# Moving TensorE's skip products and GpSimd's layer 1 constants inside a four-layer kernel's layer 0 scan

## The reference

```python
h = _layernorm(x, axis=-1) * (1 + ca) + sa
x = x + ga * mixer(h)
h = _layernorm(x, axis=-1) * (1 + cb) + sb
x = x + gb * ffn(h)
```

```python
def step(h, inp):
    u_t, dt_t, B_t, C_t = inp
    dA = jnp.exp(-dt_t[..., None] * A)
    h = dA * h + (dt_t * u_t)[..., None] * B_t[:, None, :]
    y = jnp.einsum('bdn,bn->bd', h, C_t)
    return (h, y)
_, ys = jax.lax.scan(step, h0, xs)
y = jnp.transpose(ys, (1, 0, 2)) + x * D     # the skip term
y = _bound(y)                                # clip to 0..1
y = _bound(y * silu(z))
return jnp.einsum('bld,ed->ble', y, W_out)
```

## Time and profile before

| | |
|---|---|
| median of 3 runs | 1184.9 us (1184.57 to 1188.87) |
| profiled execution | 1181.61 us |
| its span | 1180.4 us, mean granted clock 0.878 |
| PE busy | 927.2 us (79%) |
| DVE busy | 860.3 us (73%) |
| ACT busy | 621.3 us (53%) |
| POOL busy | 519.3 us (44%) |
| layer 0 scan | about 77 to 290 us of the span |

### The profile page before, as it was taken

How to read it: one execution, slowest core, us unless ns; L and a number is a source line. 1 busy time by engine, 2 the same in 40 slices (tenths; PEclk the granted TensorE clock), 3 DMA queues, 4 the chain that set the end, 5 groups by cost and what they waited for, 6 DMA issues and landing times. The chain is left out here.

```text
span 1180.4 us, 18509 instructions
## 1 busy us (share of the span) xinstructions
PE 927.2 (79%) x5579; PEld 568.8 (48%) x5579; DVE 860.3 (73%) x1655; ACT 621.3 (53%) x1344; POOL 519.3 (44%) x527
## 2 busy tenths in 40 slices
PE   5978799999657876568888888768999286767992
PEld 3523345444335552222223322347999155756982
DVE  6887999999999467878888885184544568985333
ACT  3487798896222343326776667624543293232432
POOL 2067897999401423301111111225653466235773
PEclk9978999999877988759999999859999587867996
DMA  9000000000000300411100010061110200001114
GB/s 312 1 1 1 1 1 1 1 1 1 0 1 0 143 1 28 133 28 27 27 23 21 20 29 3 1 252 36 44 37 26 75 0 1 1 36 35 50 48 121
DMA packets 28014, 46.29 MB, mean 39 GB/s; under 512 B 8720, under 2 KB 16408, under 8 KB 26896
## 3 DMA queue, kind: packets, MB, share of 16 engines
q1 hardware_dynamic: 22672, 34.66, 9.4%
q0 software_dynamic: 4096, 8.35, 2.4%
q10 hardware_dynamic: 1152, 2.10, 0.5%
HBM read 34.45 MB, written 12.58 MB: 40 GB/s over the span
## 5 line engine op out<-in xcount | busy, mean ns | idle before, releaser
L2060 DVE TENSOR_REDUCE sb_l_mxp<-ps 128x2 f32<-128x1024 f32 (+3 forms) x152 | 171.4, 1164 | 39.6 <-PE ps L1873 38.4
L1050 POOL TENSOR_TENSOR sb_gs<-sb_hs,sb_xp 128x512 f32<-128x512 f32 x128 | 162.4, 1298 | 24.2 <-PE ps L682 20.4
L2003 ACT ACTIVATE sb_l_pT<-ps 128x512 f32<-128x512 f32 (+3 forms) x256 | 111.4, 521 | 75.7 <-PE ps L1928 74.6
L682 PE MATMUL ps<-sb_gs,sb_ident 128*128 128x512 f32 x256 | 132.4, 608 | 0.2
L2996 PE MATMUL ps<-sb_hT,sb_f_shared 128*128 x936 | 121.6, 281 | 1.7 <-ACT sb_hT L3027 1.6
L2996 PEld LDWEIGHTS ps<-sb_hT,sb_f_shared 128*128 128x128 f32 x936 | 113.9, 197 | 2.8 <-issue 2.5
L1928 PE MATMUL ps<-sb_l_qk 51*128 51x512 bf16 (+3 forms) x384 | 88.1, 332 | 18.4 <-ACT sb_l_pT L2003 8.0
L3035 ACT ACTIVATE sb_f_hid<-ps 128x512 f32<-128x512 f32 x78 | 46.6, 597 | 78.9 <-PE ps L2996 78.9
L3094 POOL DMA_INDIRECT moe_y<-sb_f_rows,sb_f_rowi x64 | 64.3, 1004 | 53.4 <-DVE sb_f_rows L3066 41.0
L953 ACT ACTIVATE sb_dA<-sb_dt,sb_negA 128x512 f32<-128x512 f32 x109 | 77.7, 713 | 10.3 <-DVE sb_hs L856 9.6
L3005 PE MATMUL ps<-sb_sw_f_out,sb_f_hid 128*128 x624 | 82.5, 276 | 0.6 <-DVE sb_f_hid L3055 0.6
(11 more groups left out here) (414 smaller groups left out, 2143.4 us busy)
## 6 DMA issues: line engine op xcount, KB each, us to landing
sb_sw_f_in<-w_f_in SPq DMA_DIRECT2D x2, 2048.0 KB, 10.0
sb_sw_f_out<-w_f_out SPq DMA_DIRECT2D x2, 2048.0 KB, 12.5
sb_l_qk<-spill SPq DMA_DIRECT2D x112, 32.0 KB
spill<-sb_l_parts SPq DMA_DIRECT2D x12, 256.0 KB, 2.9
moe_y<-c_f_zero SPq DMA_DIRECT2D x1, 2048.0 KB, 9.7
sb_sw_f_up<-w_f_up SPq DMA_DIRECT2D x1, 2048.0 KB, 12.3
moe_h<-sb_f_rows SPq DMA_DIRECT2D x8, 256.0 KB, 4.7
sb_f_rows<-moe_y SPq DMA_DIRECT2D x8, 256.0 KB, 6.1
```

The source lines that it names most:

```text
L682: pe.matmul(ps[:, 4 + e * CPB + hf, :], ident[:], gs[:, p % SL, :], start=False, stop=n == DS - 1).then_inc(acc, 1)
L1050: gp.tensor_tensor(gs[:, q % SL, :], hs[:, q % SL, :], cs[:, k % 2, hf * CH:(hf + 1) * CH], ALU.mult).then_inc(times_c, 1)
L2003: ac.activation(pT[e % 3][:, h, 0:width], ps[:, bank[n_bank], 0:width], ACT.Exp, scale=L2_SCALE).then_inc(exped, 1)
L2060: dv.tensor_reduce(dst, src, AX_X, ALU.max).then_inc(max_out, 1)
```

## The change

Four things are edited. In PE's order of the scan, the skip products of batch 0 are issued earlier: those for e=0 behind the first two C rows, before the loop, and those for e=1 at q = 0 and 1; only the latter wait for DVE's dt work (`dt_out`, count 9 instead of 10). Those of batch 1 are issued behind the add of step 63, ahead of `outputs`, except that of bank 7, which stays before the add of step 67. DVE adds half 0's output to x at q = 70 instead of 69; half 1 stays at 71. POOL's layer 1 work is split: the rows part comes before the wait for `xz_mm`, the gated part behind it. The bias rows are laid out in another order (b_k, b_v, ffn bias, b_o), so that only three of the four are split into bf16 parts.

```diff
--- before.py
+++ after.py
@@ -101,7 +101,7 @@
         if name[:2] in ("w_", "c_") and name.split("_")[1] not in ("mod", "f3") and name not in late:
             w[name] = sb("s" + name, list(A[name].shape), A[name].dtype)
 
-    l1_rows3 = sb("l1_rows3", [96, 4 * D], BF16)
+    l1_rows3 = sb("l1_rows3", [96, 3 * D], BF16)
     l1_sel3 = sb("l1_sel3", [96, P], BF16)
     f0_ctx = ExitStack()
     f0_tmp = sb("f0w_tmp", [P, 2, 3 * D], ctx=f0_ctx)
@@ -584,7 +584,8 @@
             def skip_product(b, e, hf):
 
                 t0 = b * S + hf * CH
-                pe.wait_ge(dt_out, ET * NCH + 2)
+                if e > 0:
+                    pe.wait_ge(dt_out, ET * NCH + 1)
                 pe.wait_ge(l0_const, SKIP)
                 if b > 0:
                     pe.wait_ge(*y_gated[b - 1, e, hf])
@@ -666,6 +667,8 @@
                 b_row(q)
             for key in first_rows:
                 bank3 = bank3_row(key)
+                if key[0] == "c":
+                    skip_product(0, 0, key[2])
             for q in range(NQ + LAG):
                 if NB_ <= q + 2 < NQ and by_vector(q + 2):
                     b_row(q + 2)
@@ -673,14 +676,19 @@
                     product(q + 2)
                 for key in rows_at(q):
                     bank3 = bank3_row(key)
+                if q < CPB:
+                    skip_product(0, 1, q)
                 p = q - LAG
                 if p >= 0:
                     b, n, e, hf = steps[p]
-                    if n == 0:
-                        skip_product(b, e, hf)
+                    if p == per_b + per_n - 1:
+                        skip_product(1, e, hf)
                     pe.wait_ge(times_c, p + 1)
                     pe.matmul(ps[:, 4 + e * CPB + hf, :], ident[:], gs[:, p % SL, :], start=False,
                               stop=n == DS - 1).then_inc(acc, 1)
+                    if p == per_b - 1:
+                        for part in Y_ORDER[:-1]:
+                            skip_product(1, *part)
                     if p % per_b == per_b - 1:
                         bank3 = outputs(b, 0, bank3)
                         outputs(b, 1, bank3)
@@ -825,7 +833,7 @@
 
             multiply(0)
 
-            add_at = {per_b + LAG + 1 + 2 * hf: hf for hf in range(CPB)}
+            add_at = {per_b + LAG + 2 + hf: hf for hf in range(CPB)}
             for q in range(NQ + LAG):
                 if q in add_at:
                     add_outputs(0, add_at[q])
@@ -1022,8 +1030,9 @@
             for b in range(B):
                 gp.tensor_tensor(wog[:, b], wo[:], gate[:, 0, 0, b, :].unsqueeze(1).to_broadcast([P, ET, D]),
                                  ALU.mult).then_inc(gp_made, 1)
+            gpsimd_layer1_rows()
             gp.wait_ge(xz_mm, 4 * NCH)
-            gpsimd_layer1_constants()
+            gpsimd_layer1_gated()
 
             def multiply(k):
                 b, n, e, hf = steps[k * per_n + gp_step(k)]
@@ -1074,21 +1083,16 @@
     l1_const = sem("l1_const")
     ROWS3 = 2 * B + 1
 
-    def gpsimd_layer1_constants():
-        rows, wo = w["w_l1_rows"], w["w_l1_o"]
+    def gpsimd_layer1_rows():
+        rows = w["w_l1_rows"]
         gp.wait_ge(*ld["rest"])
-        gp.wait_ge(gate_ready, 1)
-        for b in range(B):
-            gp.tensor_tensor(l1_wog[:, b], wo[:], gate[:, 1, 0, b, :], ALU.mult).then_inc(l1_const, 1)
-            gp.tensor_tensor(l1_bog[:, b], rows[:, 2 * D:3 * D], gate[:, 1, 0, b, :], ALU.mult).then_inc(l1_const, 1)
         gp.memset(l1_sel3[:], 0.0).then_inc(*g_step.up())
-        gp.tensor_copy(l1_rows3[:], rows[0:96]).then_inc(*g_step.up())
+        gp.tensor_copy(l1_rows3[:], rows[0:96, 0:3 * D]).then_inc(*g_step.up())
         gp.wait_ge(*g_step.now())
-        gp.wait_ge(l1_const, 2 * B)
         for r0 in (0, 32, 64):
             gp.memset(l1_sel3[r0:r0 + 1, :], 1.0)
         for r0, rest in ((32, 1), (64, 2)):
-            part, exact = l1_rows3[r0:r0 + 32], rows[r0:r0 + 32]
+            part, exact = l1_rows3[r0:r0 + 32], rows[r0:r0 + 32, 0:3 * D]
             for _ in range(rest):
                 gp.tensor_tensor(exact, exact, part, ALU.subtract).then_inc(*g_step.up())
                 gp.wait_ge(*g_step.now())
@@ -1097,7 +1101,13 @@
                     i.then_inc(*g_step.up())
                     gp.wait_ge(*g_step.now())
         i.then_inc(l1_const, 1)
-        gp.wait_ge(l1_const, ROWS3)
+
+    def gpsimd_layer1_gated():
+        rows, wo = w["w_l1_rows"], w["w_l1_o"]
+        gp.wait_ge(l1_const, 1)
+        for b in range(B):
+            gp.tensor_tensor(l1_bog[:, b], rows[:, 3 * D:4 * D], gate[:, 1, 0, b, :], ALU.mult).then_inc(l1_const, 1)
+            gp.tensor_tensor(l1_wog[:, b], wo[:], gate[:, 1, 0, b, :], ALU.mult).then_inc(l1_const, 1)
 
     with ExitStack() as ctx:
         layer0_mixer(ctx)
@@ -1560,7 +1570,7 @@
         def tensor():
             for c in range(NCH):
                 pe.wait_ge(x_new, 2 * NCH + c + 1)
-                bias_row(4 + c, slice(3 * D, 4 * D), TPC)
+                bias_row(4 + c, slice(2 * D, 3 * D), TPC)
                 normalised(pe, 3, c)
                 for t in range(TPC):
                     i = pe.transpose(ps[:, c, t * P:(t + 1) * P], xn[:, c * TPC + t, :], ident[:])
@@ -3233,8 +3243,8 @@
     out["w_l1_q"] = T(inp["L1_attn_W_q"])
     out["w_l1_kv"] = np.ascontiguousarray(np.concatenate([inp["L1_attn_W_k"].T, inp["L1_attn_W_v"].T], 1))
     out["w_l1_o"] = T(inp["L1_attn_W_o"])
-    out["w_l1_rows"] = np.tile(np.concatenate([inp["L1_attn_b_k"], inp["L1_attn_b_v"], inp["L1_attn_b_o"],
-                                               inp["L1_ffn_bias"]]), (P, 1))
+    out["w_l1_rows"] = np.tile(np.concatenate([inp["L1_attn_b_k"], inp["L1_attn_b_v"], inp["L1_ffn_bias"],
+                                               inp["L1_attn_b_o"]]), (P, 1))
     out["w_l1_bq"] = inp["L1_attn_b_q"].reshape(P, 1)
     dec = np.exp(-np.arange(S, dtype=f) / f(S)).astype(f)
     out["c_l1_decc"] = np.ascontiguousarray(dec.reshape(TPB, P).T)
```

## The result

The changed kernel took 1178.4 us, the median of 11 runs (1174.6 to 1183.5); the kernel before, measured beside it, 1187.5 us (11 runs, 1184.6 to 1194.2). The ratio is **0.9927, 95% interval 0.9909 to 0.9946**: 0.73% faster, 6 to 11 us. The same two kernels on two other chips gave 0.9936 (0.9911 to 0.9961) and 0.9963 (0.9942 to 0.9985). The forecast was 1179.8 us, a ratio of 0.9957 to the median then known.

A forecast was written before the change was run, and what follows sets the result against it. No single engine bounds the scan; POOL paces it with DVE and PE close behind, so only holes can be won. Gains 1.7 + 0 + 3.4 = 5.1 us off the 1184.9 median gave 1179.8 us, range 1173.0 to 1186.0.

The forecast's parts named there:

- rival 1: Start of scan: clock stays high as skips fill PE's gaps; 1175.5 to 1178.6 us, say 1178.0; chance 0.30.
- my main case: Whole kernel: gains of 1.7, 0 and 3.4 us, 5.1 in all, giving 1179.8 us; chance 0.38.
- Part 3: Batch change: skips ahead of the outputs, x added one step later; gain 3.4 us.
- The lower bound, 1.9 us: Batch change: without the low clock inside the outputs, the old order would have ended them 1.5 us sooner.
- Part 1: Start of scan: batch 0's four skip products moved between the first rows; gain 1.7 us, bounds 0.4 to 2.9.
- I walk PE at the low clock: PE before step 4, timed at the low clock: step 4's b row usable at 83.85 us, 0.3 later than before.
- a stall of 1.2 us: Step 8: its b row comes at about 91.4 us where DVE wants it at 90.2.
- The lower bound of 0.4 us: Start of scan: last b row at 84.5 us and both stalls of steps 8 and 9 at low clock, 2.2 us.
- The two later waits of the five stay: Start of scan: two later DVE waits for PE's b rows, together 3.2 us, remain in the changed kernel.
- Part 2: POOL's layer 1 constants split in two, rows work moved earlier; worth 0, between -0.5 and +0.5 us.
- the collision: Before the first steps: POOL's earlier dt times u holds up DVE's own, which ends at 78.45, 0.85 us later.
- The slower rival: Scan: without the dense block of skips and adds, PE runs at 1.2 GHz until 127 us; 1192.9 us; chance 0.05.

The follow-up runs named there:

- part 2 alone: The kernel before with only POOL's layer 1 constants work split in two, rows part earlier; ratio 1.0010 (0.9993 to 1.0027).

## Why the prediction was right, and where it was off

The direction and the two places were right, and so was the size of the second; the gain was forecast at 5.1 us and is 6.7 in the scan with the early head, and 4.8, 7.0 and 9.1 between the medians of the three groups of runs. The forecast ratio, 0.9957, lies just outside the first interval (0.9909 to 0.9946) and inside the two later ones. At the start of the scan it was the mechanism of rival 1 that occurred, not that of my main case.

- **Part 3** was right step by step. Forecast: skips 0.8 us behind the gating, outputs 3.6 us, scan of 69 in the wait, POOL's hole about 5 us, 13.25 us from gating to POOL's row, a gain of 3.4. Measured: 0.82, 3.73, yes, 5.51, 13.38, and 3.4. The lower bound, 1.9 us where the old order has no dip in the outputs, was right as well: 1.8 against the trace of part 2 alone.
- **Part 1** is the term that was mis-sized: 1.7 us forecast, 3.4 measured alone. The step that was wrong is "I walk PE at the low clock". The clock was high until 86 us, the b row of step 4 was never late, and that is rival 1, to which I gave 0.30. Its other half held: "a stall of 1.2 us" at step 8 was 1.16 in one trace and 2.23 in the other, for the reason given (few rows between 84 and 87, then adds at 1.2 GHz). The lower bound of 0.4 us doesn't follow from its own terms: 84.5 + 10.75 + 2.2 is 97.45, against 97.52 a gain of 0.1.
- "The two later waits of the five stay" was half wrong: 3.2 us became one wait of about 1.7 (the 2.8 us above less 1.16). PE arrives with the clock high or back sooner and the second is gone. This and the high clock make the difference of the sum: clip to the scan of step 9 gained 2.5 us (24.3 to 21.8), clip to clip 3.7 (54.2 to 50.5). From the second clip to the gating of batch 0, 0.4 us was given back (67.7 to 68.2).
- **Part 2**: the collision was foreseen, its price nearly: DVE's product ends 4.81 us behind the start of the clip instead of 4.42, 0.4 later and not 0.85, because the clip itself became 1.22 us (it was 1.65): in every trace in which POOL's casts run beside it the clip takes 1.65 to 1.67, in every one without them 1.22. The product of step 2 came 7.24 us behind the clip, 0.24 earlier than the 7.48 of before instead of 0.25 later. That step 4's b row would hide it was wrong, since that row was early. Without the collision the scan of step 9 came 0.95 us sooner, and the lead was gone by the second clip. The value of the part, 0, stands within the ratio's interval. On DVE the moved work showed as a product of 1.85 instead of 1.22 us at 53.9, two clips of 1.63 instead of 0.75 at 57.3 and a product of 1.40 instead of 1.22 at 59.0. The next one started 60.42 instead of 59.50, nearly 1 us late, and by 65.9 the waits for ACT had taken it up.
- The slower rival (the clock never coming back without the dense block) did not occur. In the trace used above PE held the clock from 70 to 86 us. In the one with the late head it dipped earlier (0.76 and 0.74 in the two stretches from 76.2 to 83.0, 1.00 to 86.4, then 0.50 from 89.9 to 93.3) and came back within some 7 us each time.

That the measured time, 1178.4, came out so near the forecast of 1179.8 is in part luck. The kernel before had a median of 1184.9 us in the three runs that I built on and 1187.5 in eleven, 2.6 more, and the gain in that group was 9.1 instead of 5.1, 4.0 more; the two nearly cancel.

## What to carry to other kernels

Work that must be done once and has no successor for a while (a bias, a skip term, a first product of an accumulation) belongs into the in-order engine's waits before the loop, not in front of the step that needs it: what it costs is not its own time but that of everything queued behind it. Before trusting a trace's span of a kernel with runs that spread by 0.5%, compare a stretch that starts at a common event; here two traces of the changed kernel agreed to 0.2 us in the scan where their spans, on two chips, differed by 25. Ask too whether the one trace of the kernel before stands for all its executions: half of what part 3 gains is there only if the clock falls over the outputs. And an edit that shows nothing alone may be worth its part once the wait in front of it is gone: test it together with the one that moves the bound, too.

## What was not expected of the hardware

- A dip of PE's clock to 1.2 GHz between 36 and 42 us, in 6 of 14 traces, went with a start of the scan 3 us later (76 instead of 73) and with later dips at other places: the changed kernel's scan took 211.3 us with the late start and 209.0 and 209.2 with the early one.
- Filling PE's gaps held the clock (until 82.7 us instead of 76.1) and yet gained nothing, when the work behind was unchanged: 24.3 us from clip to step 9 in both.
- DVE's clip of 128x2048 f32 took 1.65 us beside POOL's casts and 1.22 without them; its dt times u of 128x1024 took 1.22 alone, 1.53 behind a POOL subtract and 2.35 behind POOL's 2.42 us product.
